# Dense edge counts for the first 6656 destinations in layers two and three of a graph network

## What is computed

```python
h = relu(layernorm(x))
# layer 0: x += segment_sum((h[src] @ W) * norm[:, None], dst)
# layer 1: x += GRU(segment_sum(MLP([h[src], h[dst], edge_attr]), dst), h)
# layer 2:
neigh = segment_sum(h[src], dst, num_segments=12500)
x += relu(((1 + eps) * h + neigh) @ W1 + b1) @ W2 + b2
# layer 3:
agg = segment_sum(h[src], dst, num_segments=12500)
x += relu((agg / max(cnt, 1)) @ W_l.T + b_l + h @ W_r.T)
```

## Time and profile before

| | us |
|---|---|
| median of 3 runs | 9328.82 (9328.22 to 9331.21) |
| span of the profiled execution | 9329.2 |
| GpSimd busy | 6576.3 (70%) |
| TensorE busy | 4953.4 (53%) |
| VectorE busy | 3646.5 (39%) |
| ScalarE busy | 1659.2 (18%) |
| DMA moved | 476.52 MB, 51 GB/s over the span |

### The profile page before, as it was taken

The page is one execution under the profiler, slowest core; times in us unless marked ns, Lnnn a source line. Parts: engine busy times, 40 slices in busy tenths (PEclk is TensorE's granted clock), DMA queues, the critical chain, the costliest instruction groups (busy, mean ns, idle before and its releaser), DMA issues. The chain is left out here.

```text
span 9329.2 us, 145773 instructions
## 1 busy us (share of the span) xinstructions
PE 4953.4 (53%) x31445; PEld 4537.8 (49%) x31446; DVE 3646.5 (39%) x7396; ACT 1659.2 (18%) x4731; POOL 6576.3 (70%) x6906
## 2 busy tenths in 40 slices
PE   6888888888676666666665222222223222222223
PEld 5777777777566666666665222222223222222223
DVE  9888888888544333333334111111113111111112
ACT  4455555555431000000002000000001000000000
POOL 3677777777426777777775777777774777777777
PEclk6666666666655555555556555555556555555555
DMA  8222222122442222222211111111111111111111
GB/s 328 53 55 55 54 55 55 54 55 54 156 151 59 42 42 43 42 42 43 42 41 27 27 27 27 27 27 27 27 27 32 27 27 27 27 27 27 27 27 37
DMA packets 528946, 476.52 MB, mean 51 GB/s; under 512 B 366105, under 2 KB 370347, under 8 KB 526812
## 3 DMA queue, kind: packets, MB, share of 16 engines
q0 software_dynamic: 212608, 218.99, 11.2%
q1 hardware_dynamic: 314328, 254.96, 9.6%
q10 hardware_dynamic: 1925, 1.58, 0.1%
HBM read 332.70 MB, written 142.29 MB: 51 GB/s over the span
## 5 line engine op out<-in xcount | busy, mean ns | idle before, releaser
L1270 POOL DMA_INDIRECT h_rows<-h_tab,idx x3322 | 3135.8, 944 | 1114.5 <-issue 1011.4
L1825 PE MATMUL ps_seg<-hot,h_rows 128*64 128x80 f32 x6656 | 987.0, 343 | 3024.2 <-DMA h_rows<-h_tab,idx 2950.9
L1825 PEld LDWEIGHTS ps_seg<-hot,h_rows 128*64 128x64 f32 x6656 | 895.9, 227 | 3134.5 <-issue 2282.1
L917 POOL DMA_INDIRECT sorted_tab<-msg,row_at x1661 | 1591.3, 958 | 660.5 <-issue 496.0
L1270 POOL DMA_INDIRECT a_rows<-a_tab,idx x1661 | 1567.9, 944 | 534.7 <-issue 505.1
L1752 DVE TENSOR_TENSOR acc_t<-acc_t,ps_seg 64x80 f32 x416 | 95.6, 230 | 3025.3 <-PE ps_seg L1825 3025.3
L807 PE MATMUL ps_at<-next_at,lo_t 128*128 128x98 f32 x3328 | 1032.5, 406 | 326.3 <-ACT next_at L870 276.6
L807 PEld LDWEIGHTS ps_at<-next_at,lo_t 128*128 128x128 f32 x3328 | 759.4, 282 | 378.1 <-issue 219.3
L835 PE MATMUL ps_msg<-u_win,hot_t 128*128 128x64 f32 x3328 | 830.6, 345 | 7.7 <-DVE hot_t L740 7.7
L1441 PE MATMUL ps_seg<-hot,act_rows 128*65 128x80 f32 x3328 | 492.2, 341 | 635.7 <-ACT act_rows L1514 635.7
L1441 PEld LDWEIGHTS ps_seg<-hot,act_rows 128*65 128x65 f32 x3328 | 448.9, 229 | 682.2 <-issue 682.2
(11 more groups left out here) (226 smaller groups left out, 7301.1 us busy)
## 6 DMA issues: line engine op xcount, KB each, us to landing
sorted_tab<-acc_t SPq DMA_DIRECT2D x16, 4030.0 KB
landed_rows<-sorted_tab SPq DMA_DIRECT2D x124, 520.0 KB
lo_row<-lo_tab SPq DMA_DIRECT2D x209, 256.0 KB
h_rows<-h_tab,idx POOLq DMA_INDIRECT x3322
ends_of<-edge_t SPq DMA_DIRECT2D x208, 132.0 KB
sorted_tab<-msg,row_at POOLq DMA_INDIRECT x1661
a_rows<-a_tab,idx POOLq DMA_INDIRECT x1661, 2.4
idx<-src_steps SPq DMA_DIRECT2D x624, 4.0 KB, 1.6
```

The costliest lines, as they stand in the source:

```text
L917: pool.indirect_dma_start(sorted_tab[:, :], bass.IndirectOffsetOnAxis(ap=row_at[:, r, k:k + 1], axis=0), msg[:, r, k, :], None).then_inc(s ...
L1270: pool.indirect_dma_start(dest[:, r, k, :], None, table[:, :], bass.IndirectOffsetOnAxis(ap=idx[:, r, k:k + 1], axis=0)).then_inc(landed[r ...
L1825: last = pe.matmul(ps_seg[0:F, b, 0, 0:W], rows_of[:, r, k, :], hot[:, b, k, :], start=(k == 0), stop=(k == K - 1))
```

## The change

**Constants and tables.** The first 6,656 destinations (`DENSE` = 208 x 32) become dense. Table `adj_tab` in DRAM holds, for every one of the 98 columns of source nodes (`JU`) and each dense destination, the number of edges between them, in bf16: 208 blocks of 128 x 98 x 32.

**A planning stage** before layer one finds where each group of four destinations begins in the edge list (`starts`, 1,664 of them), writes one record of two numbers per edge to `rec_tab` (which source node, which destination), and makes `base_far`, `meta_far` and `cumx_far`, the windows with their start moved to 6,656 at least. It also computes a flag, `is_dense`: each group has at most 128 edges, and the first 6,656 destinations fill at least 108 steps. `turns_r` is 1 with the flag and 28 without.

**In layer one** each of the 208 steps builds 32 destinations of the table: SyncE reads eight starts into a register and loads 128 records of 8 bytes for each; VectorE makes one-hots of the source row (8 x 128) and of source column and destination (8 x 392); TensorE multiplies them (eight bf16 products into `ps_adj`, two at a time between its other work); ScalarE copies each result into `adj` and stores 803 KB per step. `ps_seg` has one buffer now instead of two.

**In layers two and three** 24 turns of gathered steps (steps 112 to 207) run beside the dense products, then `turns_r` turns more. x_nm is first stored to `x_tab`, and its place holds h_nm split into two bf16 parts (`upper`), with a third in `low`. ScalarE loads pieces of `adj_tab` (16 x 128 runs of 768 bytes; 8 pieces make a block of 512 destinations) into four slots. TensorE does in each step first the sum of the gathered rows, then one piece (two in each of the first eight steps): 12 or 13 columns, each once with `upper` (128 wide) and once with `low` (64 wide), 512 columns moving. After eight pieces VectorE adds the block, times the flag, into all 128 partitions of `acc_t`; the weights `w21` and `wl3` of the following stages are laid twice above each other, so that both halves count. Own terms are done four columns a turn; the bias of layer two is added in one instruction after x_nm has been loaded back and before the last turn. The cut diff:

```diff
+DENSE = SUPERS * DSTEP
+BLOCKS = DENSE // DCOLS
+PIECE_ENDS = (0, 12, 24, 36, 48, 60, 72, 85, JU)
+UNITS_A = BLOCKS - 1
+TURNS_A = 2 * UNITS_A
+FIRST_A = TURNS - TURNS_A
+TURNS_R = 1
...
+                    for c in range(TC):
+                        dve.wait_ge(near_in[c % RING], 16 * (c // RING + 1))
+                        dve.tensor_scalar(near_below[:, c % 2, :], near[:, c % RING, :], limit[:, c:c + 1], None,
+                                          ALU.is_lt).then_inc(near_counted, 1)
+                        dve.wait_ge(near_counted, c + 1)
+                        step(dve.tensor_reduce(step_n[:, 2, c:c + 1], near_below[:, c % 2, :], AX_X, ALU.add))
...
+                            hold(sp, lo_hot, s - RING + 1)
+                            hold(sp, keyed, s - RING + 1)
+                            for k in range(GPS):
+                                at = sp.value_load(starts[0:1, bass.ds(s * GPS + k, 1)], min_val=0, max_val=N_EDGES)
+                                sp.dma_start(rec[:, r, k, :], rec_tab[bass.ds(at, P), :]).then_inc(rec_in[r], 16)
...
+                        dve.tensor_tensor(one_lo[:, b, :, :], ps_iota[:, 0:1, :].to_broadcast([P, GPS, P]),
+                                          rec[:, r, :, 1:2].to_broadcast([P, GPS, P]), ALU.is_equal).then_inc(lo_hot, 1)
...
+                        dve.tensor_tensor(one_key[:, b, half, :], key_row.to_broadcast([P, GPS // 2, KEYS]),
+                                          key_of[:, b, half, None].to_broadcast([P, GPS // 2, KEYS]),
+                                          ALU.is_equal).then_inc(key_hot, 1)
...
+                            hold(pe, adj_kept, GPS * s + k - 1)
+                            pe.matmul(ps_adj[:, k % 2, 0:KEYS], one_lo[:, b, k, :], one_key[:, b, k, :], start=True,
+                                      stop=True).then_inc(adj_done, 1)
...
+                            hold(act, adj_done, GPS * s + k + 1)
+                            nc.scalar.activation(adj[:, b, :, k * WORD:(k + 1) * WORD],
+                                                 ps_adj[:, k % 2, 0:KEYS].rearrange("p (j d) -> p j d", d=WORD),
+                                                 ACT.Copy).then_inc(adj_kept, 1)
...
+                            hold(pe, piece_in[slot], 16 * loads_of(u, g, t))
+                            if k == 0:
+                                hold(pe, dense_added, n)
+                            for j in range(low_end, high_end):
+                                pe.matmul(out_of[:, :, :], upper[:, j, :], pieces[:, slot, :, e], start=(j == 0),
+                                          stop=False, skip_group_check=True)
+                            for j in range(low_end, high_end):
+                                last = pe.matmul(out_of[0:F, :, :], low[:, j, :], pieces[:, slot, :, e], start=False,
+                                                 stop=(j == JU - 1), skip_group_check=True)
...
+                        for u in first_then_loop(pe, UNITS_A):
+                            for t in range(PIECES):
+                                if r == 1:
+                                    turn_own(i)
+                                if layer == 3 and r == 3:
+                                    own_terms(i)
+                                products(q, FIRST_A * RING + q, r, i, t % 2)
+                                for g in piece_numbers(u, t):
+                                    multiply(u, g, t)
```

More of the change, by code:

```diff
@@ L1251, in _, with gather_rows @@
                             norm.root(act, CHUNKS - 1)
-        def load_indices(sp, landed):
-            with sp.Fori(1, TURNS) as i:
-                for r in range(RING):
-                    s = RING * i + r
-                    hold(sp, landed[r], LANDED * i)
-                    sp.dma_start(idx[:, r, :], src_steps[bass.ds(s, 1), :, :].rearrange("s p k -> p (s k)")
-                                 ).then_inc(idx_in[r], 16)
-        def gather_rows(pool, layer, table, dest, landed, used):
+        def gather_rows(pool, table, dest, landed, used):
             for i in first_loop_last(pool, TURNS):
@@ L1476, in _ @@
                             last.then_inc(pre_main, 1)
+                            if not first:
+                                groups(1 - b, s - 1, 2, 4)
                             with pe.If(more > 0):
@@ new lines, in _ @@
+                        if layer == 2:
+                            add_own(TURNS_A, RING * TURNS_A)
+                            dve.wait_ge(x_back, 16)
+                            dve.tensor_tensor(x_nm[:, :, :], x_nm[:, :, :], ps_bias[:, 0:1, :].to_broadcast([P, J, F]),
+                                              ALU.add).then_inc(bias_added, 1)
+                        for i, steps in rest(dve):
+                            for r in range(RING):
+                                q, s, b = RING * TURNS_A + RING * i + r, steps[r], r % 2
+                                start_step(q, s, b)
+                                accumulate(q, s, b)
@@ L1828, in _ @@
-                                with pe.If(more > 0):
-                                    seen = before(pe, s)
-                                    with pe.Fori(0, more) as w:
-                                        hold(pe, segx_hot, seen + w + 1)
-                                        for k in range(K):
-                                            last = pe.matmul(ps_seg[0:F, b, 0, 0:W], rows_of[:, r, k, :], hot[:, b, k, :],
-                                                             start=(k == 0), stop=(k == K - 1))
-                                        last.then_inc(segx_done, 1)
@@ L1836, in _ @@
-                                pe.drain().then_inc(seg_done, 1)
+                                products(q, FIRST_A * RING + q, r, i, t % 2)
+                                for g in piece_numbers(u, t):
+                                    multiply(u, g, t)
+                        turn_own(TURNS_A)
+                        if layer == 3:
+                            own_terms(TURNS_A)
+                        for i, steps in rest(pe):
+                            for r in range(RING):
+                                products(RING * TURNS_A + RING * i + r, steps[r], r, TURNS_A + i, r % 2)
```

609 lines of the change are left out of this document (494 added, 115 removed).

## The result

The changed kernel takes 8,222.6 us (median; 8,217.7 to 8,225.0) where the kernel before takes 9,330.0 (9,328.2 to 9,338.1) beside it: ratio 0.8811, 95% interval 0.8799 to 0.8824. The forecast was 7,690 us in a range of 7,320 to 8,010, so the gain is there and 533 us smaller than forecast, and the time lies outside the range. The profiled execution spans 8,215.7 us, and the kernel before's 9,329.2.

A forecast was written before the change was run, and what follows sets the result against it. GpSimd's gathers were taken to bound layers one to three, with SyncE binding layer one after the change. 9,329.2 - 2,050 (layers two and three) + 330 + 12 (layer one) + 70 (planning) gave 7,690 us, range 7,320 to 8,010.

The forecast's parts named there:

- part 2: Layers two and three: dense products fit in 10.0 us a step; starts and ends add 58 and 50 us.
- part 4: Planning stage before layer one: VectorE's comparisons, passes and counts, DRAM round trips and barriers add 70 us (45 to 110).
- SyncE keeps up: Rival, layer one: at 0.77 us a read the step stays at 10.0 to 10.2 us; kernel 7,380 us, chance 0.24.
- GpSimd being locked out in layer one: Rival: VectorE's new one-hots shut out the gathers, 24.1 us a step; kernel 10,290 us, chance 0.02.
- SyncE's step: Layer one: eight reads at 1.11 us plus 2.7 us make 11.6 us against 10.0, +330 us over 208 steps.
- far bound of 13.7: Layer one: upper bound in us of SyncE's step, each read at 1.38 us from a gap with a branch; +770 us.
- The rest of the step: Layer one, SyncE beside the eight reads: 1.51 us of earlier work, 1.05 branch and load, 0.15 added waits; 2.7 us.
- SyncE costs more: Rival, layer one: 1.38 us a read, 13.7 us a step, +770 instead of +330 us; kernel 8,130 us, chance 0.12.
- the start: Layers two and three: first sum about 56 us in, then eight steps at 13 us; +45 us a layer (15 to 130).
- the sentence on the order: Dense steps: summing gathered rows first gives seg_done before the dense matmuls, so GpSimd's ring of four is not held up.
- The clock: Layers two and three: TensorE's granted clock rises with its busy share, 0.50 at 25% to 0.66 at 83%; step 10.0 us.
- estimate by that floor: Layer one: with a 600 ns register load, eight reads cost 7.5 us, a step about 10.2; kernel 7,400 us.

The follow-up runs named there:

- e10: Changed kernel with 64 idle SyncE instructions put once ahead of layer one's code, outside the loop: 8,045.9 us, ratio 0.8612 to the kernel before.
- e5: Changed kernel with TensorE multiplying a dense step's tables before summing its gathered rows: 8,190.2 us, ratio 0.8784 to the kernel before.
- e11: Changed kernel with 128 idle SyncE instructions put once ahead of layer one's code, outside the loop: 8,230.6 us, ratio 0.8809 to the kernel before.
- e3: Changed kernel with the bounds dropped from layer one's eight start reads a step: 7,576.4 us, ratio 0.8118 to the kernel before.
- e4: Changed kernel with acc_t cleared ahead of the splitting of h_nm in layers two and three: 8,192.6 us, ratio 0.8782 to the kernel before.

## Why the prediction was wrong

**Right: what bounds each stage.** Layers two and three remained with GpSimd, at 10.0 us a step and 1,600 gathers; 1,044 us a stretch where "about 1,040" was written. TensorE's dense step is 1.29 + 2.75 + 2.78 and its gaps, under 10 us, and it waits 1.1 to 1.75 us for the gathers. The whole of part 2 and part 4 was met: -2,042 us for the two layers and the gap between them (-2,050 forecast), +68 for the planning stage (+70).

**Right: which mechanism would cost something.** SyncE became layer one's bound, the record loads follow each other, GpSimd waits for idx. The rival "SyncE keeps up" fell, and so did the fear of GpSimd being locked out in layer one: its gathers take 0.944 us there as before.

**Wrong: the size of one term,** SyncE's step: 11.6 us forecast, 14.06 measured, and the far bound of 13.7 did not reach it. It has three parts:
- One read with its DMA: 1.11 us forecast from a gap of 0.77 us on another line, 1.27 measured as the mean of e10's steps. Eight of them give 1.3 us a step, 275 us in the layer. Somewhat less than half of that is the ordinary read (1.18 us); the rest is the one slow read of a step. The trace before had the pieces of the ordinary one: the same kinds of instruction stand there one by one with their durations, in the view by source line, and I read only the distances between DMA issues.

```profile
L597 SPq FUSED_REGOPS  x977: 37/155/189, 246.0 to 4870.0; - x196
L597 SPq TENSOR_LOAD <-meta x624: 263/276/471, 245.5 to 4869.5; - x156
L597 SPq SEQ_ASSERT  x624: 18/18/32, 246.3 to 4870.2; - x156
```

  The slow read it did not have: no register load of that line takes over 0.47 us.
- The rest of the step: 2.7 forecast; 13.23 of e10 less 8 x 1.27 leaves 3.0. 0.3 us a step, 70 us.
- The fetching of instructions: nothing forecast, 14.06 - 13.23 = 0.83 us a step measured by e10, 173 us in the layer. No row of the kernel before shows it (its page has 48 packets in SyncE's instruction queue), so it could not be priced from rows; but the forecast added some 32 reads to a loop's body and counted only their time.

275 + 70 + 173 = 518 us, against 846 - 330 = 516 us missed. The range failed with it: its upper end of 8,010 held the far bound of SyncE only in part, though the bound was a mere gap between two other instructions. The rival "SyncE costs more", 8,130 us at 0.12, was the nearest case.

**Right by luck: the start.** +45 us was made up of a first sum 56 us in and a TensorE catching up for 8 steps. The stretch is longer than 100 steps of 9.98 by 1,044 - 998 = 46 us, but it is spread over 12 steps, with 12.7 us in the fourth for the clear and 7 us at each block's end, which were put at 2.

**Wrong: the sentence on the order.** "Summing the gathered rows first" was credited with keeping the ring of four free. e5 shows that the ring does not need it: once it is full, TensorE's slack of 1 to 2 us a step covers either order, and where TensorE is late the sum first costs more, since what it waits for is queued on VectorE behind the addition of a block.

**The clock: the right step, by a reason that does not hold.** 10.0 us a step came out, and a sum that took 2.37 us now takes 1.27 to 1.29. But the prediction said that the granted clock rises with the busy share, up to 0.66 at 83%. In layers two and three TensorE is busy 74% and 77% of the windows above, less than in layer zero, at a clock of 0.87 and 0.89, so mostly the level of 2.4 GHz. So the busy share alone does not order these stages; what raised the clock was not tried. The Trainium skill (TensorE: Matmul & The Clock Gate, HAM oscillation) tells of a matmul kernel that falls back to half rate in every wait for DMA. That did not happen here, where the waits are shorter than in that kernel: with one of 1.1 to 1.75 us in each step a sum takes 1.29 us. Behind a wait of 2.74 us the next matmuls are slower, 3.56 for 2.75 us; the granted clock is 1.00 from 6086 to 6089 us and 0.61 from 6089 to 6092.

## What to carry to other kernels

An engine that only issues DMAs has a busy line too, though no page prints it: count its registers' loads, bound checks and issues (here 0.27, 0.26 and 0.33 us) for each step before giving it work, and read them in the view by source line. A loop of run-time turns whose body grows may be fetched again in every turn; look for a growing count of instruction packets and for pauses at the loop's end with no wait in them, and shorten the body (or try to move it). When two kinds of work share an engine, the order that is best in the steady state may be indifferent, and the ends of the stage decide.

## What the runs showed of the hardware

- A loop of 302 executed instructions on SyncE (366 with the skipped ones), reached at one place, costs 173 us more in 51 turns than the same loop 64 instructions further on; 128 further on, it costs as much as at first (e10, e11). The packets in the instruction queue are 313, 63 and 314.
- A register's load from SBUF on SyncE takes 0.27 us (the median of 1,664, at least 0.262). The Trainium skill (DMA: Bandwidth & Descriptors, Latency and other measured facts) gives about 600 ns as its floor; the measurement decides. The prediction's estimate by that floor, 7,400 us, is 820 us short: it has a load that is too dear, and nothing for the address and the bounds. The prediction also held that the gap of 0.77 us does not contradict the floor; the load in that gap took 0.27 us.
- One such load in each step of layer one takes about 0.9 us with no wait to be seen (e10: 1.07 a step over 0.5 us, e3: 0.11). The cause is open.
- Eight of GpSimd's gathers at the start of layer two take 1.3 to 1.6 us in place of 0.94, in step with VectorE's splitting subtractions of 1.7 to 1.8 us. GpSimd's and VectorE's timeline of the changed kernel:

```profile
6004.10 0.94 POOL L2063 DMA_INDIRECT h_rows<-h_tab,idx  x1 [0.30 <-issue]
6005.35 1.63 POOL L2063 DMA_INDIRECT h_rows<-h_tab,idx  x1 [0.30 <-issue]
6007.29 1.43 POOL L2063 DMA_INDIRECT h_rows<-h_tab,idx  x1 [0.30 <-issue]
```

```profile
6004.34 3.56 DVE L2138 TENSOR_TENSOR pieces<-h_nm,x_nm 128x1600 f32<-128x1600 f32 x2 [26.72 <-ACT x_nm L2206]
6007.82 1.82 DVE L2143 TENSOR_TENSOR low<-pieces,x_nm 128x1600 bf16<-128x1600 f32 x1
```

  In e4 the subtractions begin at 5999.16, and the slow gathers at 6000.23 with them, while the clear of 11.15 us slows none. That they move together is shown; which port or rule makes it was not tried. It costs nothing here, as the ring of four is full soon after and GpSimd waits anyway.
- That a body touching three blocks is kept, and one touching four is not, is shown for one body at three places, and agrees with five bodies of other lengths. Whether it holds on the other engines was not tried.
